# Gated cross attention with 16 heads on one core: the memory rows' projections without filler products in between

## The reference

```
x = x + tanh(g_xattn) * xattn(layernorm(x), ctx)          # x: 1 x 1024 x 128, ctx: 1 x 6404 x 128
    qp     = q @ Wq.T
    scores = qp @ kv.T                                    # 1024 x 6404
    idx    = argmax(scores, axis=-1)                      # one row of the context for each of 1024 queries
    mem    = kv[idx]                                      # 1024 x 128
    mk, mv = split(mem @ Wkv.T)                           # 8 + 8 columns, shared by all 16 heads
    out    = softmax(heads(qp) @ mk.T / sqrt(8)) @ mv     # 1024 x 1024 for each head
    return out @ Wc.T
x = x + tanh(g_ffn) * moe_ffn(layernorm(x))               # top 2 of 8 experts, 160 slots each
```

## Time and profile before

| | |
|---|---|
| three runs, us | 333.48, 337.15, 337.73 |
| median, us | 337.15 |
| the profiled execution, us | 335.67 |
| its span, first to last instruction, us | 333.9 |
| mean granted clock of PE, share of 2.4 GHz | 0.971 |

### The profile page before, as it was taken

How to read it: one execution, slowest core, us unless ns; L and a number is a source line. 1 busy time by engine, 2 the same in 40 slices (tenths; PEclk the granted TensorE clock), 3 DMA queues, 4 the chain that set the end, 5 groups by cost and what they waited for, 6 DMA issues and landing times.

```text
span 333.9 us, 5318 instructions
## 1 busy us (share of the span) xinstructions
PE 291.1 (87%) x1781; PEld 214.3 (64%) x1781; DVE 190.1 (57%) x686; ACT 155.5 (47%) x333; POOL 78.7 (24%) x165
## 2 busy tenths in 40 slices
PE   5899979999986778869999888998889997888993
PEld 2688979999985335547777666664333433357993
DVE  4585555766888777888787868220211206725344
ACT  1665543555543014757676667686314120045640
POOL 3873135465545422000000001000023000244000
PEclk9999997999999987999999999999999999689998
DMA  7832553656200000029180000100001000011002
GB/s 204 284 110 93 182 180 135 206 197 213 90 22 12 16 8 20 1 82 332 13 247 0 6 0 3 36 2 2 0 3 36 0 0 3 7 40 21 14 2 63
DMA packets 18459, 24.09 MB, mean 72 GB/s; under 512 B 2120, under 2 KB 14986, under 8 KB 18426
## 3 DMA queue, kind: packets, MB, share of 16 engines
q1 hardware_dynamic: 16836, 20.39, 18.3%
q0 software_dynamic: 1184, 3.14, 4.1%
q10 hardware_dynamic: 406, 0.16, 0.2%
HBM read 12.62 MB, written 10.93 MB: 71 GB/s over the span
## 4 chain that ended last, share of the span: by engine, by line
PE 59%; DVE 17%; DMA 8%; issue 6%; ACT 4%; POOL 4%; SPq 0%; DVEq 0%; ACTq 0%; POOLq 0%
PE ps L1417 8%; PE ps L1472 7%; PE ps L1526 6%; DVE mx L1093 4%; PE ps L1504 4%; PE ps L1365 4%; PE ps L1367 3%; PE ps L1366 3%; PE ps L1326 3%; PE ps L1644 3%; DMA pair<-in_ctx_dram,at 3%; PE ps L1650 3%; PE ps L1673 2%; PE ps L1412 2%; DVE kv_nat L1084 2%
## 5 line engine op out<-in xcount | busy, mean ns | idle before, releaser
L937 DVE CUSTOM_DVE_ANT_0 kv_nat<-ps,gain 128x400 f32<-128x400 f32 (+1 forms) x64 | 36.3, 573 | 22.1 <-PE ps L1367 19.8
L1365 PE MATMUL ps<-shared,q_hi 128*128 128x400 f32 (+1 forms) x128 | 46.9, 367 | 2.0 <-DVE best L937 1.2
L697 ACT ACTIVATE gain<-ps 128x400 f32<-128x400 f32 (+1 forms) x64 | 32.3, 505 | 32.5 <-PE ps L1367 32.2
L1093 DVE TENSOR_REDUCE mx<-ps 128x1 f32<-128x384 f32 x84 | 40.9, 546 | 9.6 <-PE ps L1504 9.5
L1367 PE MATMUL ps<-shared,q_lo 128*128 128x400 f32 (+1 forms) x128 | 44.8, 350 | 0.0
L1366 PE MATMUL ps<-shared,q_hi 128*128 128x400 f32 (+1 forms) x128 | 44.7, 349 | 0.0
L803 ACT ACTIVATE kv_nat<-ps 128x512 f32<-128x512 f32 x72 | 39.3, 602 | 9.0 <-PE ps L1526 8.2
L1526 PE MATMUL ps<-q_rows,k_blk 128*128 128x256 f32 x192 | 39.9, 300 | 2.6 <-DVE mx L1084 1.7
L1526 PEld LDWEIGHTS ps<-q_rows,k_blk 128*128 128x128 f32 x192 | 31.5, 190 | 8.0 <-issue 2.9
L1504 PE MATMUL ps<-k_blk,q_rows 128*128 128x384 f32 x84 | 28.5, 365 | 1.5 <-DVE mx L1093 1.4
L609 POOL TENSOR_TENSOR rstd<-var_eps,minus_half 128x4 f32<-128x4 f32 x2 | 2.1, 1032 | 114.1 <-DVE var_eps L1124 114.1
(11 more groups left out here) (297 smaller groups left out, 509.8 us busy)
## 6 DMA issues: line engine op xcount, KB each, us to landing
m_rows<-kv_nat SPq DMA_DIRECT2D x48, 201.0 KB, 2.1
kv_nat<-in_ctx_dram SPq DMA_DIRECT2D x5, 640.0 KB, 9.6
ew_sb<-in_L_ffn_eW_dram SPq DMA_DIRECT2D x1, 2048.0 KB, 10.2
rw_sb<-in_L_ffn_rW_dram SPq DMA_DIRECT2D x1, 1024.0 KB, 5.4
x_sb<-in_x_dram SPq DMA_DIRECT2D x2, 256.0 KB, 3.9
xn_rows<-xn SPq DMA_DIRECT2D x2, 256.0 KB, 2.3
out_dram<-fin SPq DMA_DIRECT2D x4, 128.0 KB, 1.9
rw_sb<-in_L_ffn_rW_dram SPq DMA_DIRECT2D x1, 256.0 KB, 2.9
```

Of the source, the lines that this page charges most:

```text
L697: act.activation(gain[:, m % 3, 0:end - start], ps[:, b:b + end - start], ACT.Relu).then_inc(s_rl, 1)
L937: dve.tensor_tensor_reduce(out=m_all[b2][:, start:end], in0=ps[:, b:b + end - start], in1=gain[:, m % 3, 0:end - start], scale=1.0, scalar ...
L1093: dve.tensor_reduce(to, sc, AX.X, ALU.max).then_inc(s_p1u, 1)
L1365: pe.matmul(o, q_h, hi, start=True, stop=False)
```

## The change

PE's loop becomes one tile after the other: turn, wait for ACT's copy, project. The two fillers behind each projection are gone. ACT's loop has T instead of T + 1 rounds: copy t, key block t-1, wait for projection t, round t. Before it was copy t, round t-1, key block t-2. The seven fillers behind L1453 stay. DVE's and POOL's code is unchanged.

```diff
--- before.py
+++ after.py
@@ -743,20 +743,17 @@
                     act.copy(k_blk[block2, 2, c], k_dense[block2, c]).then_inc(s_kb_act, 1)
 
                 act.wait_ge(s_kz, 1)
-                for t in range(T + 1):
-                    if t < T:
-                        act.wait_ge(s_mT, t + 1)
-                        act.copy(memT[:, t * P:(t + 1) * P], ps[:, (t % 2) * HALF:(t % 2) * HALF + P]).then_inc(s_mTs, 1)
+                for t in range(T):
+                    act.wait_ge(s_mT, t + 1)
+                    act.copy(memT[:, t * P:(t + 1) * P], ps[:, (t % 2) * HALF:(t % 2) * HALF + P]).then_inc(s_mTs, 1)
                     if t:
-
-                        act.wait_ge(s_mkv, t)
-                        if t >= 3:
-                            act.wait_ge(s_kdn, t - 2)
-                        b = 2 + (t - 1) % 2
-                        act.activation(k_a[:, (t - 1) % 2, :], ps[:, b * HALF:b * HALF + P], ACT.Identity,
-                                       scale=k_sgn[:, 0:1], bias=k_one[:, 0:1]).then_inc(s_ka, 1)
+                        key_block(t - 1)
+                    act.wait_ge(s_mkv, t + 1)
                     if t >= 2:
-                        key_block(t - 2)
+                        act.wait_ge(s_kdn, t - 1)
+                    b = 2 + t % 2
+                    act.activation(k_a[:, t % 2, :], ps[:, b * HALF:b * HALF + P], ACT.Identity,
+                                   scale=k_sgn[:, 0:1], bias=k_one[:, 0:1]).then_inc(s_ka, 1)
                 act.wait_ge(s_kdp, 1)
                 act.activation(kd_a[:, 0:T * P // 2], ps[:, 0:T * P // 2], ACT.Identity, scale=k_sgn[:, 0:1]
                                ).then_inc(s_kda, 1)
@@ -1426,23 +1423,16 @@
                 last.then_inc(s_xT, 1)
 
             def attention_pe(T):
-                for t in range(T + 1):
-                    if t < T:
-                        pe.wait_ge(s_mem[t % 4], 16 * (t // 4 + 1))
-                        if t >= 2:
-                            pe.wait_ge(s_mTs, t - 1)
-                        pe.transpose(ps[:, (t % 2) * HALF:(t % 2) * HALF + P], mem[:, t, :], ident[:]).then_inc(s_mT, 1)
-                    if t:
-                        k = t - 1
-                        pe.wait_ge(s_mTs, t)
-                        if k >= 2:
-                            pe.wait_ge(s_kdn, k - 1)
-                        else:
-                            pe.wait_ge(s_idxc, 1)
-                        b = (2 + k % 2) * HALF
-                        pe.matmul(ps[:, b:b + P], wk_rep[:].rearrange("p j r -> p (j r)"), memT[:, k * P:(k + 1) * P],
-                                  start=True, stop=True).then_inc(s_mkv, 1)
-                        keep_clock(6, 2, all_b)
+                pe.wait_ge(s_idxc, 1)
+                for t in range(T):
+                    pe.wait_ge(s_mem[t % 4], 16 * (t // 4 + 1))
+                    pe.transpose(ps[:, (t % 2) * HALF:(t % 2) * HALF + P], mem[:, t, :], ident[:]).then_inc(s_mT, 1)
+                    pe.wait_ge(s_mTs, t + 1)
+                    if t >= 2:
+                        pe.wait_ge(s_kdn, t - 1)
+                    b = (2 + t % 2) * HALF
+                    pe.matmul(ps[:, b:b + P], wk_rep[:].rearrange("p j r -> p (j r)"), memT[:, t * P:(t + 1) * P],
+                              start=True, stop=True).then_inc(s_mkv, 1)
                 for k in range(T):
                     bv = 4 * HALF + k * DH
                     last = pe.matmul(ps[:, bv:bv + DH], memT[:, k * P:(k + 1) * P], consts[:, C_WKV + DH:C_WKV + 2 * DH],
```

## The result

Slower, where a small gain was forecast. Over 20 executions each the change's median is 339.75 us (335.19 to 343.95) and the kernel before's is 335.06 us (333.42 to 337.91). The ratio is **1.0108, 95% interval 1.0077 to 1.0139**, so 3.6 us. It leaves out executions over 1.5% above the fastest of their kernel, 8 of the change's 20 and none of the kernel before's, and is therefore smaller than the quotient of the medians (1.0140, 4.7 us). The range of the prediction (333.0 to 338.0) does not hold 339.75.

A forecast was written before the change was run, and what follows sets the result against it. PE was taken as the bound, through its chain of waits in the memory rows; DVE's data coming 0.9 us earlier gave 335.67 - 0.9 = 334.8 us, for the median 337.15 - 0.9 = 336.2 us, range 333.0 to 338.0.

The forecast's parts named there:

- The other branches: Branches for four and eight tiles: not run, so no term of the sum.
- Rival A: Memory rows: fillers were in the way, low clock ends by 131.4 us; -0.9 us, the forecast itself, chance 0.45.
- B: Memory rows: clock returns later, seven fillers at half clock become the bound; +0.25 to +0.6 us, chance 0.25.
- The terms at the low clock: Memory rows: projection's start to rounding 0.66 us, six value products 0.7; if slow, L1453 0.65 and seven fillers 3.0.
- The third landing: Third tile's gather: issued at 125.17 us, landed 2.6 us later, at 127.8.
- ACT's order: Third tile: copy now stands behind rounding 1 on ACT, costing about 0.2 us.
- The hand-over from ACT's copy to the projection: Memory rows: PE's wait ending in ACT's copy, taken as 0.05 us, bounds 0.02 and 0.30.
- DVE's first dense keys: First tile: dense keys of tile 0 come at 127.35 to 127.70 us, 0.7 us earlier.
- The second place: Fifteen fillers at 288.20 us, 6.13 us at low clock: up to 1.5 us either way, no sign given.
- The base: Starting median of the kernel before, 337.15 us from three executions, from which 0.9 us was taken.

The follow-up runs named there:

- x2: Kernel before with 92 more fillers in the never-run branch for eight tiles, moving the exit to 9182; 337.59 us, ratio 1.0084.
- x1: The change with 36 more fillers in the never-run branch for eight tiles, putting the exit back at 8998; 335.45 us, ratio 1.0037.
- z1: The change's orders with two fillers kept behind each projection and six more ahead of the memory rows, exit at 8998; ratio 0.9971.
- y2: The change with two instead of seven fillers behind the difference product, exit at 8998; 335.94 us, ratio 1.0041.
- x3: Kernel before, old PE and ACT orders, without the two fillers behind each projection, exit kept at 8998; 336.09 us, ratio 1.0038.
- y3: The change with six more fillers ahead of the memory rows, where PE waits for the first gather, exit at 8998; ratio 1.0000.
- y6: Kernel before with six more fillers ahead of the memory rows, where PE waits for the first gather, exit at 9010; ratio 1.0012.
- x4: The change's PE and ACT orders with the two fillers kept behind each projection, exit at 8998; 336.43 us, ratio 1.0033.

## Why the prediction was wrong

- **The other branches.** "The other two branches (four and eight tiles) are not run" stood in the sum as 0. That step failed, and it made most of the loss. Their code is 58 instructions shorter, and together with the 14 in the branch that is run this moved the exit to 222 behind a multiple of 256 in PE's program, close to the edge of a fetched block. Measured by x2: 1.0084, 2.8 us; by the change over x1: 2.4 us. No rival held it.
- **Rival A, "the low clock ends by 131.4 us".** It failed. In the change it ended 11.6 us behind the third gather (133.8 - 122.2), on the scale of the earlier trace rows at about 136.8. B was the case that happened, at 0.25 against 0.45. My argument against it, that PE is dense from 128.8 on, was no argument: in the change PE has no gap from 126.2 us on, and the clock still came back only at 133.8, 7.6 us later. And the premise of A, that the fillers were in the way, failed with it. z1 has all of them, and with the clock at 1.00 its L1488 comes 7.4 us behind the gather, which is the distance that I forecast for their removal (8.3 - 0.9). In y2, without pairs and at the low clock, the data alone bring that product at 8.2 us, a gain of 0.1.
- **The terms at the low clock.** A projection's start to rounding: 127.04 - 126.21 = 0.83 us, taken 0.66. My row had the clock's return in its middle, but that isn't the reason: the other two projections of the kernel before ran wholly at 0.50 and took 0.67 (128.98 - 128.31) and 0.69 us (127.46 - 126.77). The likely reason is the pause ahead of it. Before, PE loaded the projection's weights 0.2 us ahead of its start, under the turn; in the change, behind the wait for ACT's copy, load and product start together (timelines, before and after):

```profile
128.11 0.54 PEld L1443 LDWEIGHTS ps<-kv_nat,wk_rep 128*128 128x128 f32 x2
128.31 0.64 PE L1443 MATMUL ps<-kv_nat,wk_rep 128*128 128x128 f32 x2
...
126.21 0.50 PEld L1434 LDWEIGHTS ps<-kv_nat,wk_rep 128*128 128x128 f32 x2 [0.65 <-ACT kv_nat L748]
```

  Six value products: 1.08, taken 0.7, close to the upper bound of 1.14. L1443: 0.84, taken 0.65. The seven fillers: 2.99, as worked out.
- **The third landing.** Taken 2.6 us behind its issue, the median of three; in the change it took 3.1, and the chain runs through it. That is 0.5 us that the forecast lacks. The 0.2 us that it charged for ACT's order were not paid (rounding 1 ends at 125.68, and the third copy starts at 125.89, behind its turn).
- **What B's price left out.** I put +0.4 us on it, read at L1497's line, where +0.8 were measured. But the maximum products, too, run at the low clock until 133.8 us, so that 1.5 us are missing at the first logits. The memory rows' share is 1.0037 by x1 and 1.0038 by x3, 1.2 us.
- **What held.** The hand-over from ACT's copy to the projection: 124.39 behind 124.34, 0.05 us as taken. DVE's first dense keys came 4.8 us behind the first gather's issue in place of 5.5, 0.7 us sooner, as taken.
- **The second place.** Its fifteen fillers took 6.10 us in the change, 6.13 before: no part of this loss.
- **The base.** The forecast of 336.2 us stands on a median of 337.15 us, taken from three executions. Over 20 it is 335.06, 2.1 us less. So the miss of 3.6 us in the number flatters the forecast: from the right base it would have been 334.2 and the miss 5.6 us.

The two parts make 2.4 to 2.8 and 1.2 us, 3.6 to 4.0, against 3.6 measured. By the medians it is 3.2 (x2) and 1.0 us (x1), against 4.7.

## What to carry to other kernels

An edit in a part that every branch has moves the code behind the branches; compare the engine's idle "issue" time at the exit of a branch before blaming the edit, and test it with instructions that are never executed. Fillers that stand in the chain of waits are not free to remove: ask what the clock will be, and how far into the next stage it stays there. Fillers placed where the engine waits anyway cost nothing that these ratios show (y3, y6), but they held the clock only together with those in the gaps.

## What the runs showed of the hardware

- After a taken jump of PE two 16 KB fetches of instructions start 3.0 to 3.5 us apart, in every kernel here. With eight products (3.5 us) queued and a target 38 or 242 behind a multiple of 256 of PE's program nothing is seen of it; at 222 PE stands still for 2.3 to 2.6 us, until 2.5 to 2.7 us behind the start of the second fetch.
- Behind that pause the clock fell in both profiled executions that have it, and in none of the other twelve: 0.50 from 253.4 to 256.7 us in the change, which cost 2.0 us more there (seven products in 4.98 us; in the 16 before, seven take 3.0).
- Value products 8 columns wide double with the clock as well: 0.57 us for six at 1.00, 1.08 at 0.50.
- With pauses of PE of 0.35 to 0.41 us in each tile the clock was not back for 10 us in x4, though two fillers stood in each tile; in the earlier trace rows it was back after 3.3 us without a gap. In the change PE had no gap for 7.6 us before it was back. Why it took that long is open.
